# Attention and a routed feed-forward block on one core: a new order of score steps, first loads on GpSimd's queue, the guard as a bias column in one unit

## The chip, the core and the metric

The kernel runs on one core of a Trainium2 chip. A core has five engines with queues of their own: TensorE (PE, matmuls into PSUM), VectorE (DVE), ScalarE (ACT), GpSimd (POOL) and SyncE (SP), which here only issues DMAs. They meet at semaphores. A DMA is issued by SyncE or GpSimd and carried out by 16 DMA engines. The metric is the device time of one execution in microseconds (us).

## The reference

Four sequences of 1024 tokens, 256 channels. All inputs and the result are float32.

```python
qkv = x @ W_attn.T + b_attn                      # x: (4, 1024, 256)
q, k, v = split(qkv)                             # 16 heads of 16 channels
att = q @ k.T / sqrt(16) + rel_emb[bucket(distance)]
att = softmax(where(causal, att, -inf))
x = layernorm(x + (att @ v) @ W_proj.T + b_proj)
# then: gate scores pick one of 2 experts per token,
# relu(x @ w1[e] + b1[e]) @ w2[e] + b2[e], plus the term of the expert not picked (its input is zero)
# plus a shared expert; result = layernorm(x + sum)
```

The distance bias differs from a constant only where query and key are less than 256 apart, so it has to be added only in blocks near the diagonal.

## The kernel before

**Projection (project_in).** x comes in eight tiles of 512 tokens (two per sequence, t = 0 and 1). TensorE turns a tile (L644, from x_in), ScalarE and VectorE split it into a high and a low part (L491, L535), TensorE forms four blocks c of q and k from three products (L701) and then v (L663). ScalarE and VectorE split each q/k block into parts (L510, L581). SyncE stores the parts of a tile with four DMAs to qk_d in DRAM (store_tile, L412). GpSimd multiplies the high parts of q and k (selfs, L475), and one tile later TensorE sums squares and products into norms (L654, L656). parts has two buffers: before ScalarE writes a tile into one, the stores of the tile two earlier must have landed.

SyncE's queue is in order. For each tile n it issues the x load of tile n + 2 (L422, 512 KB), the four stores of tile n (2 MB together), and for tiles 1 to 4 two pieces of the skewed bias table bias_t (skew_bias, L406; 16 partitions, 256 rows of 1 KB each). After tiles 3 and 5 it loads the first two stacks (first_stack): a stack holds k in k_st and q in q_first or q_second for one unit of four heads, two sides of four DMAs (load_parts, L252 to L255), 32 or 16 partitions each, and two guard rows (load_guard, L272). first_stack first waits until all stores so far have landed.

**The guard.** From the norms and the largest bias the kernel derives a number that is subtracted from every score, so that no exponential overflows. VectorE writes it to neg_guard. In the first AP_UNITS units (2) of sequence 0 it goes into the exponential as a per-partition bias operand (L1061); in all others it lies in two extra rows of q, which are read from guard_d, and the exponential has no operand (L1059). guard_d is filled from guard_fill (L447, L449); for the first AP_UNITS units it holds zeros. The last tile's stores stand behind this fill and behind a branch that is decided on VectorE (ready.decided): an exact search for maxima, which is not taken with these inputs.

**Attention (attend).** 16 units: four sequences b by four groups g of four heads. A unit runs NSTEP = 9 steps, each with two pairs of heads. A step is one or two blocks (half of the queries, key block j, first query q, width w, column) that fill 512 columns for each head of the pair. For a pair, TensorE writes the scores to one of three PSUM slots (scores, L1151); if the step has a block near the diagonal, VectorE adds bias_t there, one instruction for each such block (L1117); ScalarE takes the exponential of 128 x 1024 values into probs; and TensorE multiplies by v and sums into o_ps (outputs, L1170). TensorE runs the scores two steps ahead. The steps' blocks are listed by hand in STEPS (L57 to L59). VectorE also copies each finished half of o_ps to o_sb (evacuate, L1078), at the places EVAC1 and EVAC0 (L902).

**Division and feed-forward.** The row sums are inverted (L1085), spread by DMA, and GpSimd multiplies y_t by them, one instruction per sequence (division.batch, L1230). That of the last sequence runs in the feed-forward stage, where ScalarE needs it for tile 6. There, TensorE forms the hidden layer (L2027) and the output (L2044), ScalarE and VectorE split the hidden layer (L1753, L1757, L1935: h_lo), VectorE computes the gate scores (L1784, an operation of x1 and gate_r, both in SBUF), GpSimd adds the residual's bias row (L1288) and scatters rows by indirect DMA (L1669).

## Time and profile before

| | us |
|---|---|
| median of 3 runs | 833.5 (833.4 to 835.99) |
| the profiled execution | 833.7 |
| its span, first to last instruction | 832.0 |
| PE busy | 777.1 (93%) |
| ACT busy | 542.7 (65%) |
| DVE busy | 514.6 (62%) |
| POOL busy | 243.5 (29%) |
| mean granted clock of TensorE | 0.976 of full speed |

Shares of the whole span mix three stages with different limits: the projection ends near 110 us, attention near 395, the rest is feed-forward. So the table only says where to look; which engine sets the pace is read stage by stage. A timeline row gives the start, the duration of a run of like instructions, the engine, the line of the kernel, what is written and read, the count, and in brackets the idle time before it with what ended that time.

### The profile page before, as it was taken

How to read it: one execution, taken by the hardware profiler on the slowest of the kernel's cores; microseconds unless marked ns; L12 is line 12 of the kernel's file. 1: busy time of each engine (PE TensorE's matmuls, PEld its weight loads, DVE VectorE, ACT ScalarE, POOL GpSimd, SP SyncE). 2: the span in 40 equal slices, each digit the busy share in tenths (PEclk: the TensorE clock that was granted, in tenths of full speed). 3: DMA queues.
4: the chain of work that ended last, by engine and by line, in shares of the span. 5: the costliest groups of instructions: out<-in, count | busy, mean ns of one | idle time of the engine just before them, and what ended most of it. 6: DMA issues, size and time to landing. Idle time of an engine off the chain costs nothing.

```text
span 832.0 us, 15414 instructions
## 1 busy us (share of the span) xinstructions
PE 777.1 (93%) x5761; PEld 556.8 (67%) x5761; DVE 514.6 (62%) x1120; ACT 542.7 (65%) x698; POOL 243.5 (29%) x199
## 2 busy tenths in 40 slices
PE   7994879999999999999979999999999999999993
PEld 6884633333334333343869988989899989999993
DVE  4662556666676666766886887886735445544453
ACT  5552659999999999999435556543444555555552
POOL 6221510000020021036154453443433232233332
PEclk9997979999999999999989999999999999999997
DMA  8899975577796699791582111201285334444300
GB/s 233 230 278 217 212 233 91 92 114 117 127 183 115 118 171 159 135 170 20 105 274 64 65 52 59 71 26 53 86 304 197 121 130 168 170 178 163 140 26 29
DMA packets 57878, 114.33 MB, mean 137 GB/s; under 512 B 7971, under 2 KB 35016, under 8 KB 55496
## 3 DMA queue, kind: packets, MB, share of 16 engines
...
## 4 chain that ended last, share of the span: by engine, by line
PE 74%; DVE 10%; ACT 7%; issue 4%; DMA 3%; POOL 1%; SPq 0%; POOLq 0%; DVEq 0%; ACTq 0%
PE slots L2027 19%; PE o_ps L1170 12%; PE slots L1151 11%; PE slots L2044 10%; PE o_ps L2044 10%; PE slots L701 4%; ACT probs L1059 4%; DVE slots L1117 3%; PE slots L1392 2%; ACT probs L1061 2%; DMA x_in<-L_attn_x 2%; PE o_ps L663 2%; DVE junk L1784 2%; PE slots L644 1%; DMA qk_d<-parts 1%
## 5 line engine op out<-in xcount | busy, mean ns | idle before, releaser
L1059 ACT ACTIVATE probs<-slots 128x1024 f32<-128x1024 f32 x252 | 237.6, 1037 | 5.6 <-DVE slots L1117 4.8
L1117 DVE TENSOR_TENSOR slots<-slots,bias_t 128x512 f32<-128x512 f32 (+1 forms) x288 | 160.3, 605 | 83.8 <-PE slots L1151 82.9
L1935 DVE TENSOR_TENSOR h_lo<-h_f,h_hi 128x512 fp32r<-128x512 f32 (+1 forms) x136 | 95.9, 706 | 106.5 <-PE o_ps L2044 62.4
L1170 PE MATMUL o_ps<-probs,v_st 128*32 128x512 f32 (+3 forms) x1664 | 154.6, 472 | 1.8 <-ACT probs L1059 0.4
L1753 ACT ACTIVATE h_f<-slots,b_cur 128x512 f32<-128x512 f32 (+1 forms) x72 | 47.9, 665 | 88.0 <-PE slots L2027 81.9
L1753 ACT ACTIVATE h_f<-slots,b_c 128x512 f32<-128x512 f32 x64 | 44.0, 687 | 73.6 <-PE slots L2027 65.4
L1757 ACT ACTIVATE h_hi<-h_f 128x512 fp32r<-128x512 f32 (+1 forms) x136 | 84.3, 620 | 4.3
L1151 PEld LDWEIGHTS slots<-q_first,k_st 50*128 50x128 f32 x416 | 34.7, 188 | 65.6 <-ACT probs L1059 43.5
L1151 PE MATMUL slots<-q_first,k_st 50*128 50x512 f32 (+3 forms) x416 | 69.0, 399 | 7.7 <-ACT probs L1059 2.7
L1151 PEld LDWEIGHTS slots<-q_second,k_st 50*128 50x128 f32 x416 | 34.0, 184 | 62.1 <-ACT probs L1059 44.4
L1170 PEld LDWEIGHTS o_ps<-probs,v_st 128*32 128x32 f32 x1664 | 39.9, 109 | 49.5 <-issue 30.2
L1151 PE MATMUL slots<-q_second,k_st 50*128 50x512 f32 (+3 forms) x416 | 67.7, 390 | 4.1 <-ACT probs L1059 2.6
L1708 POOL DMA_INDIRECT out<-o_out,id_i x32 | 35.7, 1116 | 103.3 <-DVE o_out L1899 96.0
L998 POOL COPY v_st<-v_all 128x512 f32<-128x512 f32 x16 | 9.8, 623 | 177.9 <-PE o_ps L1170 173.8
L1669 POOL DMA_INDIRECT base_d<-base,slot_i x32 | 40.9, 1279 | 48.1 <-DVE base L1877 40.4
L1669 POOL DMA_INDIRECT xs_d<-x,slot_i x32 | 34.3, 1073 | 62.5 <-DVE slot_i L1815 55.0
L2044 PE MATMUL slots<-shared_hi,h_hi 128*128 128x256 f32 x128 | 38.1, 298 | 6.4 <-DVE h_lo L1935 6.4
L2027 PE MATMUL slots<-x1t_lo,cur_hi 128*128 128x512 f32 (+1 forms) x144 | 43.3, 382 | 0.0
L2027 PE MATMUL slots<-x1t_hi,cur_lo 128*128 128x512 f32 (+1 forms) x144 | 43.3, 382 | 0.0
L2027 PE MATMUL slots<-x1t_hi,cur_hi 128*128 128x512 f32 (+1 forms) x144 | 43.2, 381 | 0.0
L2027 PE MATMUL slots<-x1t_hi,shared_hi 128*128 128x512 f32 x128 | 40.5, 398 | 1.2 <-ACT x1t_hi L1322 1.2
L2044 PE MATMUL slots<-experts_hi,h_hi 128*128 x144 | 41.2, 286 | 0.2
...
## 6 DMA issues: line engine op xcount, KB each, us to landing
...
```

What stands on the lines that cost most here:

```text
L701: ins = pe.matmul(slots[:, 1 + c // 2, c % 2], wq[w][:, kc, P * c:P * c + P], xt[a][:, t, kc, :], start=(i == 0 and kc == 0), stop=(i == 2 ...
L1059: nc.scalar.activation(dst, src, ACT.Exp).then_inc(exped, 1)
L1117: ins = dve.tensor_tensor(tile, tile, bias_t[:, h0:h0 + 2, first:first + w], ALU.add)
L1151: ins = pe.matmul(slots[:, k % SLOTS, h, col:col + w], k_st[at:at + KROWS, buf, pair, P * j:P * j + P], q_st[buf][at:at + KROWS, pair, q0: ...
L1170: ins = pe.matmul(o_ps[32 * j2:32 * j2 + 2 * D, half, q:q + w], v_st[:, g, j, j2, :], probs[:, (k + j2 // 2) % PBUFS, j2 % 2, col:col + w] ...
L1669: pool.indirect_dma_start(rows[:, :], bass.IndirectOffsetOnAxis(slot_i[:, t % 2, k:k + 1], 0), src[:, k, :], None).then_inc(done, 16)
L1708: pool.indirect_dma_start(out_rows[:, :], bass.IndirectOffsetOnAxis(id_i[:, j % 2, k:k + 1], 0), (o_out if j < EXP_TILES - 1 else y2)[:, k ...
L1753: nc.scalar.activation(h_f[:, q % 2, 0:w], l1_bank[q % 2][:, 0:w], ACT.Relu, bias=bias).then_inc(hf_ok, 1)
L1757: nc.scalar.activation(h_hi[:, n % 3, 0:w], h_f[:, q % 2, 0:w], ACT.Copy).then_inc(hh_ok, 1)
L1935: dve.tensor_tensor(h_lo[:, n % 3, 0:w], h_f[:, q % 2, 0:w], h_hi[:, n % 3, 0:w].bitcast(F32), ALU.subtract).then_inc(hl_ok, 1)
L2027: ins = pe.matmul(l1_bank[q % 2][:, 0:P * blocks(u)], w1_of(u, w)[:, kc, P * q:P * q + P], (xt_hi, xt_lo)[a][:, kc, 0:P * blocks(u)], star ...
L2044: ins = pe.matmul(acc_bank[k], (h_hi, h_lo)[a][:, n % 3, P * k:P * k + P], w2_chunk(u, w, q, e), start=(q == 0 and i == 0), stop=(q == HC ...
```

## The change

Five things are changed.

1. STEPS has a new order. Blocks of keys 1 and 2 of the second half are cut in 384 and 128 queries (LONG, SHORT), and no step holds two blocks near the diagonal any more. Nine steps stay nine. The place of EVAC0 moves one step ahead.
2. The bias pieces and the first two stacks are issued by GpSimd, between its products: four pieces after tiles 1 and 2, one side of a stack after tiles 3, 4, 5 and 6. They count on semaphores of their own (first_ld). SyncE's wait for the stores ahead of a stack goes; GpSimd waits for nothing new but pool_set, guard_out and dist_out.
3. AP_UNITS is 1: unit 1 has its guard in the extra rows.
4. Unit 1's guard rows are loaded by SyncE behind the fill of guard_d, after a wait for it (ready.guard_rows), in front of the last tile's stores.
5. The division of the last sequence is four instructions instead of one. Its reader waits for all four.

```diff
-STEPS = [[WHOLE[1][1]], [WHOLE[1][3]], [WHOLE[1][2]]] + [[x] for x in WHOLE[0]]
-STEPS += [[WIDE[0], NARROW[0]], [WIDE[1], NARROW[1]]]
-STEPS += [[MIDDLE[0], FAR_LEFT], [WHOLE[1][4]], [MIDDLE[1], FAR_RIGHT]]
+LONG, SHORT = ([(1, j, q, w, q) for j in (1, 2)] for q, w in ((0, TT - P), (TT - P, P)))
+STEPS = [[WHOLE[1][3]]] + [[x] for x in WHOLE[0]] + [[NARROW[0], LONG[0]], [MIDDLE[0], FAR_LEFT], [WIDE[0], SHORT[0]]]
+STEPS += [[WHOLE[1][4]], [MIDDLE[1], FAR_RIGHT], [WIDE[1], SHORT[1]], [NARROW[1], LONG[1]]]
...
-AP_UNITS = 2
+AP_UNITS = 1
...
-                    if 1 <= n <= P // SKEW // 2:
-                        skew_bias((2 * n - 2, 2 * n - 1))
-            def first_stack(g, b):
-
-                for t in range(TPB):
-                    sp.wait_ge(stored[t], 16 * NC * b)
...
-            body(0, False, True)
-            body(1, True, True)
-            first_stack(0, 2)
-            body(2, True, True)
-            first_stack(1, 3)
-            body(B - 1, True, False)
+            batches(sp, B - 1, body)
             sp.wait_ge(ready.fill, 2)
...
+            sp.wait_ge(ready.guard_rows, 32 * GUARD)
+            load_guard(sp, guard_d, 0, AP_UNITS, q_second, ready.guard_rows)
             sp.wait_ge(ready.decided, 1)
             store_tile(B - 1, TPB - 1)
 
         def gpsimd(pool):
+            def skew_bias(pieces):
+
+                pool.wait_ge(dist_out, 16)
+                for a in pieces:
+                    skew = bass.AP(bias_rows.tensor, P - SKEW * a, [[3 * P * H - 1, SKEW], [3 * P, H], [1, WIN]])
+                    pool.dma_start(bias_t[SKEW * a:SKEW * a + SKEW], skew).then_inc(bias_in, 16)
+
+            def first_stack(g, side):
+
+                q_st = (q_first, q_second)[g]
+                load_side(pool, *unit_rows(qk_d, 0, g), k_st[:, g], q_st, first_ld[g], side)
+                if side and g < AP_UNITS:
+                    load_guard(pool, guard_d, 0, g, q_st, first_ld[g])
+
+            def queue_loads(n):
+
+                if n in (1, 2):
+                    skew_bias(range(4 * n - 4, 4 * n))
+                if n == 3:
+                    pool.wait_ge(pool_set, 4)
+                    pool.wait_ge(guard_out, 16)
+                if 3 <= n < 7:
+                    first_stack((n - 3) // 2, (n - 3) % 2)
...
                         pool.tensor_tensor(selfs[:, c], parts[:, t, c, 0].bitcast(F32),
                                            parts[:, t, KC + c, 0].bitcast(F32), ALU.mult).then_inc(self_ok, 1)
+                    queue_loads(n)
...
-        EVAC1, EVAC0, INVERT = (1, 1), (NSTEP - 1, 1), (0, 1)
+        EVAC1, EVAC0, INVERT = (1, 1), (NSTEP - 2, 1), (0, 1)
...
-                    pe.wait_ge(st_ld[buf], 16 * ST_DMAS * (2 * b + g // 2 + 1))
+                    if first and g == AP_UNITS:
+                        pe.wait_ge(ready.guard_rows, 32 * GUARD + 32)
+                    if first and g < 2:
+                        pe.wait_ge(first_ld[buf], 16 * (ST_DMAS - GUARD * g))
+                    else:
+                        pe.wait_ge(st_ld[buf], 16 * ST_DMAS * (2 * b + g // 2))
...
-        y = y_t[:, :, bass.ds(b * T, T)]
-        pool.tensor_tensor(y, y, rs_row[:, :, :], ALU.mult).then_inc(step.y_norm, 1)
+        if b < B - 1:
+            y = y_t[:, :, bass.ds(b * T, T)]
+            pool.tensor_tensor(y, y, rs_row[:, :, :], ALU.mult).then_inc(step.y_norm, 1)
+            return
+        for t in range(TPB):
+            for kc in range(KC):
+                y = y_t[:, kc, bass.ds(b * T + TT * t, TT)]
+                ins = pool.tensor_tensor(y, y, rs_row[:, kc, TT * t:TT * t + TT], ALU.mult)
+                ins.then_inc(step.y_norm, 1)
```

Where the change moves instructions, their order was listed engine by engine. First SyncE's queue in the projection, from the stores of tile 3 on, before (qk_d<-parts are a tile's stores, bias_t<-bias_rows the bias pieces, the other qk_d rows a stack):

```order
L412 DMA qk_d<-parts 128x2x512 x4
L406 DMA bias_t<-bias_rows 16x16x256 x2
L252 DMA k_st<-qk_d 32x2x1024
L253 DMA k_st<-qk_d 16x2x1024
L254 DMA q_first<-qk_d 16x2x1024
L255 DMA q_first<-qk_d 32x2x1024
L252 DMA k_st<-qk_d 32x2x1024
L253 DMA k_st<-qk_d 16x2x1024
L254 DMA q_first<-qk_d 16x2x1024
L255 DMA q_first<-qk_d 32x2x1024
L272 DMA q_first<-guard_d 2x2x1024 x2
L422 DMA x_in<-L_attn_x 128x4x256
```

The same place of the changed kernel, from the stores of tile 3 to the end of the projection:

```order
L411 DMA qk_d<-parts 128x2x512 x4
L421 DMA x_in<-L_attn_x 128x4x256
L411 DMA qk_d<-parts 128x2x512 x4
L421 DMA x_in<-L_attn_x 128x4x256
L411 DMA qk_d<-parts 128x2x512 x8
L428 DMA guard_d<-guard_fill 128x96
L430 DMA guard_d<-guard_fill 128x3x128
L428 DMA guard_d<-guard_fill 128x96
L430 DMA guard_d<-guard_fill 128x3x128
L278 DMA q_second<-guard_d 2x2x1024 x2
L411 DMA qk_d<-parts 128x2x512 x4
```

Tile 6's x (the first L421) now follows tile 3's stores at once; only two small loads are new, in front of the last stores.

Second, GpSimd in the projection of the changed kernel, from its products of tiles 0 and 1 on (before, the products stood there alone):

```order
L482 TENSOR_TENSOR selfs<-parts 128x512 x4
L443 DMA bias_t<-bias_rows 16x16x256 x4
L482 TENSOR_TENSOR selfs<-parts 128x512 x2
L443 DMA bias_t<-bias_rows 16x16x256 x4
L482 TENSOR_TENSOR selfs<-parts 128x512 x2
L258 DMA k_st<-qk_d 32x2x1024
L259 DMA k_st<-qk_d 16x2x1024
L260 DMA q_first<-qk_d 16x2x1024
L261 DMA q_first<-qk_d 32x2x1024
L482 TENSOR_TENSOR selfs<-parts 128x512 x2
```

Between the two products of one tile and those of the next there are now four DMAs (six after tile 4).

Third, VectorE through one unit of attention before, from the copy of the unit before to the copy of its own first half and on to the next unit's:

```order
L1078 COPY o_sb<-o_ps 128x512
L1117 TENSOR_TENSOR slots<-slots,bias_t 128x2x256 x3
L1117 TENSOR_TENSOR slots<-slots,bias_t 128x2x128
L1117 TENSOR_TENSOR slots<-slots,bias_t 128x2x256
L1117 TENSOR_TENSOR slots<-slots,bias_t 128x2x128
L1117 TENSOR_TENSOR slots<-slots,bias_t 128x2x256
L1117 TENSOR_TENSOR slots<-slots,bias_t 128x2x128
L1117 TENSOR_TENSOR slots<-slots,bias_t 128x2x256
L1117 TENSOR_TENSOR slots<-slots,bias_t 128x2x128
L1117 TENSOR_TENSOR slots<-slots,bias_t 128x2x256 x6
L1078 COPY o_sb<-o_ps 128x512
L1117 TENSOR_TENSOR slots<-slots,bias_t 128x2x128 x2
```

The same engine and place of the changed kernel:

```order
L1086 COPY o_sb<-o_ps 128x512
L1125 TENSOR_TENSOR slots<-slots,bias_t 128x2x128 x2
L1125 TENSOR_TENSOR slots<-slots,bias_t 128x2x256 x10
L1086 COPY o_sb<-o_ps 128x512
L1125 TENSOR_TENSOR slots<-slots,bias_t 128x2x128 x4
L1125 TENSOR_TENSOR slots<-slots,bias_t 128x2x256 x2
```

There are 18 bias instructions in a unit as before, but now one for each of the 18 pairs; before, four pairs had two and four had none.

## Rows read from the trace of the kernel before

**Rows 1.** Windows: span, busy us (count) of PE, PEld, DVE, ACT, POOL; PEclk, DMA share, GB/s.

```profile
150.00:395.00 245.00, 236.82 (x2206) 94.72 (x2206) 162.80 (x284) 238.47 (x253) 39.67 (x24) 1.00 0.75 129
```

**Rows 2.** Waits of PE in 0 to 112 us: total, times, longest.

```profile
PE slots L644 <- DMA x_in<-L_attn_x: 15.4, 2, 10.6
```

**Rows 3.** Windows of 5 us in the projection.

```profile
55.00:60.00 5.00, 5.00 (x35) 4.46 (x33) 1.37 (x3) 3.97 (x6) 1.28 (x1) 1.00 1.09 360
...
70.00:75.00 5.00, 0.00 (x0) 0.00 (x0) 0.00 (x0) 0.00 (x0) 0.00 (x0) 0.74 1.05 138
```

**Rows 4.** Timeline of SyncE's queue (SPq).

```profile
52.47 1.03 SPq L406 DMA_DIRECT2D bias_t<-bias_rows  x2
60.34 0.32 SPq L252 DMA_DIRECT2D k_st<-qk_d  x1
```

**Rows 5.** The chain that ended last, 0 to 130 us: start, us, what.

```profile
37.50 0.87 PE slots L644 x8
38.38 2.81 PE o_ps L663 x24
...
64.62 13.45 DMA x_in<-L_attn_x
...
78.11 1.97 PE slots L644 x8
80.08 4.04 PE o_ps L663 x24
```

**Rows 6.** Timeline of GpSimd in the projection.

```profile
50.11 1.30 POOL L475 TENSOR_TENSOR selfs<-parts 128x512 bf16<-128x512 f32 x1 [1.90 <-ACT parts L510]
56.94 1.28 POOL L475 TENSOR_TENSOR selfs<-parts 128x512 bf16<-128x512 f32 x1 [5.53 <-ACT parts L510]
...
102.89 1.14 POOL L1276 DMA_DIRECT2D b_c<-L_ffn_sb  x1
```

**Rows 7.** Timeline of ScalarE at the start of attention.

```profile
111.31 1.11 ACT L1061 ACTIVATE probs<-slots,neg_guard 128x1024 f32<-128x1024 f32 x1 [2.56 <-PE slots L1151]
...
114.85 4.13 ACT L1061 ACTIVATE probs<-slots,neg_guard 128x1024 f32<-128x1024 f32 x4 [0.97 <-DVE slots L1117]
...
122.56 28.44 ACT L1061 ACTIVATE probs<-slots,neg_guard 128x1024 f32<-128x1024 f32 x28 [0.27 <-DVE slots L1117]
```

**Rows 8.** Timeline of one unit of attention, ScalarE, VectorE and TensorE.

```profile
174.05 3.95 ACT L1059 ACTIVATE probs<-slots 128x1024 f32<-128x1024 f32 x4 [0.18 <-DVE slots L1117]
...
177.10 3.39 DVE L1117 TENSOR_TENSOR slots<-slots,bias_t 128x512 f32<-128x512 f32 x6 [0.16 <-PE slots L1151]
...
178.17 13.07 ACT L1059 ACTIVATE probs<-slots 128x1024 f32<-128x1024 f32 x14 [0.17 <-DVE slots L1117]
178.55 0.50 PE L1151 MATMUL slots<-q_second,k_st 50*128 50x256 f32 x4
...
180.68 0.91 PE L1151 MATMUL slots<-q_second,k_st 50*128 50x512 f32 x4
...
181.22 1.30 DVE L1117 TENSOR_TENSOR slots<-slots,bias_t 128x512 f32<-128x512 f32 x2 [0.73 <-PE slots L1151]
...
184.47 0.91 PE L1151 MATMUL slots<-q_first,k_st 50*128 50x512 f32 x4
...
191.41 1.03 ACT L1059 ACTIVATE probs<-slots 128x1024 f32<-128x1024 f32 x1 [0.17 <-DVE slots L1117]
```

**Rows 9.** Timeline of the feed-forward stage, GpSimd, VectorE and TensorE.

```profile
421.02 4.67 POOL L1230 TENSOR_TENSOR y_t<-y_t,rs_row 128x2048 f32<-128x2048 f32 x1 [23.09 <-DMA rs_row<-rsum_d]
...
421.14 4.83 DVE L1784 CUSTOM_DVE_ANT_0 junk<-x,gate_r 128x256 f32<-128x256 f32 x1
...
426.01 2.44 DVE L1784 CUSTOM_DVE_ANT_0 junk<-x,gate_r 128x256 f32<-128x256 f32 x1
...
428.49 0.42 DVE L1784 CUSTOM_DVE_ANT_0 junk<-x,gate_r 128x256 f32<-128x256 f32 x1
...
430.05 0.58 PE L2044 MATMUL slots<-shared_hi,h_hi 128*128 128x256 f32 x1 [5.17 <-DVE h_lo L1935]
```

44 lines of the change are left out of this document (18 added, 26 removed).

## The prediction

> **What bounds the kernel now.** I read the windows by stage first, then the waits, then the chain. There are three stages: projection to about 110 us, attention to 395, feed-forward to 832. In attention ScalarE is busy 238.5 of 245 us, more than any engine [rows 1], so its exponentials set the pace there and every microsecond that they wait is lost. In the projection TensorE sets the pace, 10.0 us per tile, and waits long only once: 10.6 us, for an x tile [rows 2]. That is a matter of the DMA: it moves 360 GB/s while whole tiles are stored, but 138 GB/s, just as busy, while narrow loads are in its queue (the skewed bias with 16 partitions, the stacks with 16 or 32) [rows 3]. Feed-forward is TensorE's but for one place, where it waits 5.17 us for VectorE [rows 9].
>
> **Term 1, SyncE's queue in the projection.** SyncE has issued tile 3's stores and two bias pieces by 53.5, then stands until 60.3, until those stores have landed, because the first stack reads what was stored [rows 4]. It issues the ten DMAs of that stack, then tile 6's x at 64.6, which lands 13.45 us later, behind the stack [rows 5]. TensorE wanted it at 67.5 (78.11 - 10.6). Its clock then comes back late: 0.74 granted in the window inside the stall [rows 3], the turn takes 1.97 for 0.87 and the values 4.04 for 2.81 [rows 5]. The stall costs 10.6 + 1.1 + 1.2 = 12.9 us.
>
> After the change x of tile 6 can be issued at about 52.5, right behind tile 3's stores. But what GpSimd issues instead must still be moved. By shapes, a bias piece is 0.26 MB, one side of a stack 0.79 MB, a tile's stores and x together 2.6 MB. At the rates of [rows 3] that is 1.9, 5.7 and 7.3 us of DMA (5.8 for the stores, 1.5 for x). GpSimd issues four bias pieces (7.6 us of DMA) after tiles 1 and 2 each, and one side after each of tiles 3 to 6. With SyncE's 7.3 us this makes 13 to 15 us of work in every 10 us, so both queues stay backlogged from about 31.4 us on (tile 1's products end there, 20 us before tile 3's [rows 6]). If each gets half of the time, SyncE's work up to tile 6's x (stores of tiles 2 and 3, three x: 16.0 us, and some 1.5 left over) ends at 31.4 + 2 x 17.5 = 66.4, in time. Tile 7's x is 7.3 us of work later: 81.0, for 77.5. The stores of tiles 3 to 5 land up to 5 us after ScalarE wants to overwrite their buffer; TensorE needs those results only a step later, which covers most. So 3.5 us of the 12.9 stay, and the term is **-9.4**. Bounds: all 12.9 gone; or nothing, if GpSimd's work always goes first: eight pieces and three sides are 32.3 us, and 31.4 + 32.3 + 24.8 = 88.5 puts tile 7's x 11 us late, the stall of now.
>
> GpSimd's own time is hidden while four issues fit its pauses around the two products of a tile, 5.53 and 1.90 us [rows 6]. A DMA issued there took 1.14 us (1024 elements of 4 bytes; no row has one of these shapes): four are 4.6, the six with guard rows 6.8. With that cover gone, TensorE's norms wait for the products (rival C).
>
> **Term 2, start of attention.** VectorE is free for a bias only some 0.4 us before 114.85, after its branch. Now step 0 needs no bias: its two activations run from 111.31, and only the third waits for VectorE [rows 7]. Afterwards step 0 has a bias block too, so those two come behind 114.85: 2 x 1.11 = **+2.2**. Bounds: +1 (there are gaps behind the third that may absorb some) and +3.5 (TensorE idles longer and its clock rises later).
>
> **Term 3, the bias operand is gone in unit 1.** With it 28 activations took 28.44 us, (28.44 - 1.1)/27 = 1.012 us each [rows 7], so a unit of 18 takes 18.2 us. Unit 1 then runs as in term 4, 16.85: **-1.35**. Unit 0 stays at 18.2.
>
> **Term 4, the new order of steps, units 2 to 15.** A unit takes 17.36 us (174.05 to 191.41). Its last 14 activations follow each other at (13.07 - 1.03)/13 = 0.926 us, the first four at (3.95 - 1.03)/3 = 0.973, and two waits of 0.17 end on VectorE, each costing 1.03 + 0.17 - 0.926 = 0.27 [rows 8]. That is 0.14 + 0.54 lost; without them a unit takes 16.67. The cause is seen on VectorE: from 177.10 six instructions take 3.39 us, two of 0.65 and between them the two blocks of each pair of a double step, so 1.04 a pair [rows 8], more than ScalarE's 0.926. Afterwards every pair has one block, 0.65 at most. Against it: now all nine steps pass VectorE, where two did not. The ring of three slots bounds that: from one step's first scores (180.68) over bias, exponential, the next step's second pair and the sums to the first scores two steps on (184.47) is 3.79 us [rows 8], so nine such steps are 17.06. Three of the nine have the short 128-wide block, two of them behind the copies out of o_ps. I take the middle of 16.67 and 17.06, 16.85: 0.51 x 14 = **-7.1**. Bounds: 14 x 0.30 = 4.2 and 14 x 0.69 = 9.7. TensorE gets 8 more score matmuls and 8 more output matmuls a unit, of the same columns in all. A pair of four score matmuls occupies 0.50, a pair of two 0.45 [rows 8], so 2 steps x 2 pairs x 0.05 = 0.2 us a unit, hidden while ScalarE binds, 3.2 us in all if not.
>
> **Term 5, the last division in four.** GpSimd's division begins at 421.02; VectorE's gate operation, begun 0.12 later, takes 4.83 instead of 0.42, the next 2.44 beside GpSimd's residual [rows 9]. One operation slips in behind each GpSimd instruction. With four parts of about 1.2, one gate operation passes behind each, and only h_lo meets the residual: TensorE would get h_lo about 1 us earlier. Since that hangs on the phase, I take **-0.5**, bounds -1.5 and +1. The Trainium skill (SBUF — State Buffer, Who interferes with whom) says that when VectorE reads two SBUF inputs and GpSimd reads SBUF, the one that comes later "fully blocks" for the other's whole instruction. The row agrees for VectorE; if GpSimd too were held by each of four gate operations, the residual would end 1.7 us later, and this term would be +0.4.
>
> At nothing: unit 1's guard rows and tile 7's stores behind them. Their readers, the scores of unit 1 and the stacks of unit 2, come a unit later and more (over 16 us); what is queued behind SyncE's wait is only that.
>
> **Sum.** -9.4 + 2.2 - 1.35 - 7.1 - 0.5 = -16.2. The profiled execution took 833.7 (its span 832.0), the median of the runs is 833.5: **817.5**, a span of about 816.
>
> **Rivals.** *A, the DMA work binds, not its order.* The narrow loads are the same bytes; if theirs go first, term 1 is nil: 833.7 - 6.7 = 827. For it: 138 GB/s while they move, at a full DMA share. Against: half of the time is enough for SyncE. The Trainium skill (DMA: Bandwidth & Descriptors, Issuing engines are not separate DMA queues) says that DMAs issued by different engines end on the same 16 DMA engines and that issuing from several saves only the time to issue. By it, A and 827; the projection's trace has one queue and can't tell. *B, the loop over VectorE binds attention.* If a unit stays at 17.36, terms 3 and 4 shrink to -0.85: 825.1. For it: VectorE is now in every step. Against: the loop of 3.79. *A and B together:* 834.6, no change. *C, slower: GpSimd's issue time.* If such a DMA holds GpSimd for c us, a tile needs 4c + 2.6 us there, and TensorE's norms wait from c = 1.85 on. Six such tiles lose 6 x (4c - 7.4); from c = 2.65 the whole is slower than before by over 2.5 us, at c = 2.9 it is 843. The 1.14 speaks against it; the 256 runs of 1 KB in a bias piece are its case. *D, the change does more:* both bounds good, 810.
>
> **Chances.** Forecast 0.62 (its own range 811 to 823), A 0.16, B 0.11, A and B 0.04, C 0.05, D 0.02. The range, 810.5 to 827, takes in A and B. A measurement tells about 0.3%, 2.5 us, from no change. Faster by more: 0.91 (forecast, A, B, D); within it: 0.04; slower: 0.05.
>
> **What would show it.** Term 1: TensorE's wait for x_in is 3 us or less and SyncE no longer waits for stores; in A the wait stays near 10; in C TensorE's norms wait for selfs. Term 2: the first exponential starts with the first bias, near the end of the branch. Term 4: 16.7 to 17.1 us a unit, and ScalarE's waits on VectorE shorter. Term 5: gate operations of about 1.3 us beside each part. The forecast is wrong if two DMA queues side by side move less than one after the other, or if a unit takes over 17.1.

## The result

The changed kernel takes 828.36 us (median of 20 runs), the kernel before 834.19 us beside it (20 runs): 5.8 us less by the medians. The means, 830.2 and 834.1, are 3.9 us apart, and the ratio is theirs: 0.9953, interval [0.9934, 0.9972]. The forecast was 817.5, 16 us less, and the range ended at 827.0, so the time lies above it. The runs of the changed kernel fall into two groups: 16 between 826.7 and 831.8 us, 4 between 835.5 and 836.9. Its profiled execution, with a span of 834.1 us, is one of the second group, and part of what follows is why. One run of h4_both below took 1209.9 us at a mean granted clock of 0.557, where all others of this study have 0.97 to 0.98, and is left out.

Attention as a whole, in the view of windows, beside [rows 1]:

```profile
150.00:395.00 245.00, 239.97 (x2542) 107.22 (x2544) 161.85 (x283) 237.70 (x253) 38.70 (x23) 0.99 0.78 129
```

TensorE has gone from 236.8 to 240.0 us of 245, with 336 more matmuls; ScalarE's busy time is what it was.

**The projection**, beside [rows 2] to [rows 5]: TensorE's wait for x over the same 0 to 112 us (total, times, longest), its chain, and what GpSimd issued.

```profile
PE slots L652 <- DMA x_in<-L_attn_x: 13.0, 2, 8.1
```

```profile
41.70 23.18 DMA x_in<-L_attn_x
64.89 0.04 issue
64.94 1.97 PE slots L652 x8
66.91 4.17 PE o_ps L671 x24
```

```profile
30.57 2.54 POOL L443 DMA_DIRECT2D bias_t<-bias_rows  x4
...
40.59 2.25 POOL L443 DMA_DIRECT2D bias_t<-bias_rows  x4
...
50.60 0.56 POOL L258 DMA_DIRECT2D k_st<-qk_d  x1
```

The stall has only moved by one tile: x of tile 5, issued at 41.70, landed 23.18 us later, and TensorE waited 8.1 us for it instead of 10.6 for tile 6. The slow restart (1.97 and 4.17 us) is the one of [rows 5]. GpSimd took 0.6 us to issue a DMA, far from the 1.85 at which it would have mattered: rival C is out.

The x load was not alone in being late. ScalarE stood still longer than TensorE, for the stores of tile 2, before it could write tile 4's parts into the same buffer; the prediction had allowed up to 5 us for such waits, and for tiles 3 to 5 alone. SyncE's stores of tile 3 (SPq is SyncE's queue) stretched over it.

```profile
63.63 0.69 ACT L518 ACTIVATE parts<-slots,qk_bias 128x512 fp32r<-128x512 f32 x1 [13.69 <-DMA qk_d<-parts]
```

```profile
44.38 15.82 SPq L411 DMA_DIRECT2D qk_d<-parts  x4
```

How much of the 8.1 us would have gone with x alone in time, no run shows.

**Attention**, beside [rows 7] and [rows 8]: ScalarE's timeline from the start to the end, then VectorE's copy in it, and the chain just ahead of that copy.

```profile
111.73 6.14 ACT L1069 ACTIVATE probs<-slots,neg_guard 128x1024 f32<-128x1024 f32 x6 [5.98 <-DVE slots L1125]
119.17 2.12 ACT L1069 ACTIVATE probs<-slots,neg_guard 128x1024 f32<-128x1024 f32 x2 [1.31 <-DVE slots L1125]
122.19 2.12 ACT L1069 ACTIVATE probs<-slots,neg_guard 128x1024 f32<-128x1024 f32 x2 [0.90 <-DVE slots L1125]
125.30 8.14 ACT L1069 ACTIVATE probs<-slots,neg_guard 128x1024 f32<-128x1024 f32 x8 [1.00 <-DVE slots L1125]
133.29 134.55 ACT L1067 ACTIVATE probs<-slots 128x1024 f32<-128x1024 f32 x142
271.20 3.77 ACT L1067 ACTIVATE probs<-slots 128x1024 f32<-128x1024 f32 x4 [3.36 <-DVE slots L1125]
276.43 1.94 ACT L1067 ACTIVATE probs<-slots 128x1024 f32<-128x1024 f32 x2 [1.46 <-DVE slots L1125]
279.10 115.61 ACT L1067 ACTIVATE probs<-slots 128x1024 f32<-128x1024 f32 x122 [0.73 <-DVE slots L1125]
```

```profile
270.13 0.69 DVE L1086 COPY o_sb<-o_ps 128x512 f32<-128x512 f32 x1 [3.67 <-DMA sums<-o_sb]
```

```profile
257.76 12.25 DMA sums<-o_sb
```

142 activations in a row take 134.55 us: (134.55 - 1.03)/141 = 0.947 us each, 17.04 us a unit of 18. At 271.20 that row breaks. At the start of the third sequence VectorE's copy of half 0 stands 3.67 us for the DMA that takes the row sums out of the buffer it writes, and the biases behind it on VectorE stand too. Without the break the activation of 279.10 would have come at 133.29 + 148 x 0.947 = 273.4: 5.7 us are lost. The prediction did not have this wait at all. The change asks for this copy one step earlier (NSTEP - 2 for NSTEP - 1), in a unit that is shorter.

**Feed-forward**, beside [rows 9]: the division in four, VectorE's gate operations beside it, and TensorE's next work.

```profile
421.53 5.78 POOL L1249 TENSOR_TENSOR y_t<-y_t,rs_row 128x512 f32<-128x512 f32 x4 [22.55 <-DMA rs_row<-rsum_d]
```

```profile
421.82 1.52 DVE L1804 CUSTOM_DVE_ANT_0 junk<-x,gate_r 128x256 f32<-128x256 f32 x1
...
423.38 1.39 DVE L1804 CUSTOM_DVE_ANT_0 junk<-x,gate_r 128x256 f32<-128x256 f32 x1
```

```profile
430.40 0.58 PE L2064 MATMUL slots<-shared_hi,h_hi 128*128 128x256 f32 x1 [4.85 <-DVE h_lo L1955]
```

**Where the time of the profiled execution went.** Points in the two traces: the matmul that spreads the top norms (end of the projection's critical part), 105.28 before and 102.28 after; the first activation of unit 1, 132.69 (122.56 + 10 x 1.012) and 133.29; TensorE's first matmul behind attention, 395.10 and 395.77; the matmul above, 430.05 and 430.40; the end, 832.0 and 834.1.

| term | forecast | this profile | how |
|---|---|---|---|
| 1, projection | -9.4 | -3.0 | 102.28 - 105.28 |
| 2, start of attention | +2.2 | +3.6 | 31.01 - 27.41 from the top norms to unit 1 |
| 3, unit 1 without the operand | -1.35 | -1.2 | 17.04 for 18 x 1.012 |
| 4, the other 14 units | -7.1 | -4.5 | 14 x (17.04 - 17.36) |
| wait for the sums | none | +5.7 | above |
| 5, division | -0.5 | -0.3 | 34.63 - 34.95 from attention's end to h_lo |
| rest of feed-forward | 0 | +1.8 | 403.7 - 401.9 |

The sum is +2.1, the difference of the two spans. Whether the last row is the change's is open. In the profiles below the same stretch takes 401.6 to 402.4 us in the three with the old order of steps (e3, e4, h1), and 401.6 to 404.8 in those with the new one, three of which (f3, g1, g2) lie at 401.6 to 401.8. The first row varies too, from 101.1 to 104.6 us in seven profiles with these loads, so it is taken from several profiles below.

### The profile page after: what moved, and what is told of

Its sections match the earlier page's. It is cut to its first block, busy times and chain, and to the rows that moved or that the text cites. A ratio compares the mean times of both kernels' runs of the same rounds, so it can differ in the third digit from the quotient of the medians.

```text
span 834.1 us, 16183 instructions
## 1 busy us (share of the span) xinstructions
PE 783.3 (94%) x6145; PEld 571.4 (69%) x6145; DVE 516.6 (62%) x1120; ACT 540.0 (65%) x698; POOL 258.0 (31%) x228
## 4 chain that ended last, share of the span: by engine, by line
PE 78%; DVE 8%; DMA 5%; ACT 4%; issue 3%; POOL 1%; SPq 0%; POOLq 0%; DVEq 0%; ACTq 0%
PE slots L2047 19%; PE o_ps L1183 15%; PE slots L1164 13%; PE slots L2064 10%; PE o_ps L2064 10%; PE slots L709 4%; DMA x_in<-L_attn_x 3%; PE slots L1412 2%; ACT probs L1067 2%; PE o_ps L671 2%; DMA sums<-o_sb 1%; DVE junk L1804 1%; DVE slots L1125 1%; DVE h_lo L1955 1%; PE slots L652 1%
## 5 line engine op out<-in xcount | busy, mean ns | idle before, releaser
L1067 ACT ACTIVATE probs<-slots 128x1024 f32<-128x1024 f32 x270 | 254.3, 1032 | 7.2 <-DVE slots L1125 5.6
L1125 DVE TENSOR_TENSOR slots<-slots,bias_t 128x512 f32<-128x512 f32 (+1 forms) x288 | 163.5, 607 | 92.7 <-PE slots L1164 88.7
L1955 DVE TENSOR_TENSOR h_lo<-h_f,h_hi 128x512 fp32r<-128x512 f32 (+1 forms) x136 | 99.9, 737 | 106.3 <-PE o_ps L2064 56.5
L1183 PE MATMUL o_ps<-probs,v_st 128*32 128x384 f32 (+3 forms) x1920 | 158.1, 439 | 0.5 <-ACT probs L1067 0.3
L1164 PEld LDWEIGHTS slots<-q_first,k_st 50*128 50x128 f32 x480 | 39.1, 193 | 61.3 <-ACT probs L1067 37.3
L1183 PEld LDWEIGHTS o_ps<-probs,v_st 128*32 128x32 f32 x1920 | 47.2, 110 | 46.3 <-issue 29.1
L1164 PEld LDWEIGHTS slots<-q_second,k_st 50*128 50x128 f32 x480 | 37.8, 186 | 57.5 <-ACT probs L1067 44.5
L1164 PE MATMUL slots<-q_first,k_st 50*128 50x128 f32 (+3 forms) x480 | 71.2, 382 | 6.3 <-ACT probs L1069 3.2
L1164 PE MATMUL slots<-q_second,k_st 50*128 50x128 f32 (+3 forms) x480 | 69.2, 372 | 4.1 <-ACT probs L1067 2.7
L518 ACT ACTIVATE parts<-slots,qk_bias 128x512 fp32r<-128x512 f32 x32 | 21.9, 685 | 32.8 <-PE slots L709 18.7
```

Of the source, the lines that this page charges most:

```text
L1067: nc.scalar.activation(dst, src, ACT.Exp).then_inc(exped, 1)
L1125: ins = dve.tensor_tensor(tile, tile, bias_t[:, h0:h0 + 2, first:first + w], ALU.add)
L1164: ins = pe.matmul(slots[:, k % SLOTS, h, col:col + w], k_st[at:at + KROWS, buf, pair, P * j:P * j + P], q_st[buf][at:at + KROWS, pair, q0: ...
L1183: ins = pe.matmul(o_ps[32 * j2:32 * j2 + 2 * D, half, q:q + w], v_st[:, g, j, j2, :], probs[:, (k + j2 // 2) % PBUFS, j2 % 2, col:col + w] ...
L1955: dve.tensor_tensor(h_lo[:, n % 3, 0:w], h_f[:, q % 2, 0:w], h_hi[:, n % 3, 0:w].bitcast(F32), ALU.subtract).then_inc(hl_ok, 1)
```

## The experiments

**Parts of the change by themselves.** Four kernels: the order of steps, everything but the early copy, the loads, the division.

e1_steps, the kernel before with

```
+LONG, SHORT = ([(1, j, q, w, q) for j in (1, 2)] for q, w in ((0, TT - P), (TT - P, P)))
+STEPS = [[WHOLE[1][3]]] + [[x] for x in WHOLE[0]] + [[NARROW[0], LONG[0]], [MIDDLE[0], FAR_LEFT], [WIDE[0], SHORT[0]]]
+STEPS += [[WHOLE[1][4]], [MIDDLE[1], FAR_RIGHT], [WIDE[1], SHORT[1]], [NARROW[1], LONG[1]]]
-        EVAC1, EVAC0, INVERT = (1, 1), (NSTEP - 1, 1), (0, 1)
+        EVAC1, EVAC0, INVERT = (1, 1), (NSTEP - 2, 1), (0, 1)
```

> The kernel before with the new order of steps alone (and the copy of half 0 one step earlier, as the change has it). Theory 1, TensorE is the new bound: a unit of attention takes 17.05 us as in the changed kernel (17.36 before), TensorE being busy over 99% of it, because two steps of a unit now have four score matmuls a pair for two. 14 x 0.31 = -4.3 us, the start of attention +3.6, so about -0.7 us, or up to +7 where the copy of half 0 at the start of the third sequence waits for the sums' DMA. Theory 2, the forecast's: 16.85 us a unit and +2.2 at the start, -4.9 us in all. The end of the projection (first matmul that spreads the top norms, 105.28 us before) stays where it was in both.

Measured: 832.32 us (828.9 to 836.5), ratio 0.9968 [0.9946, 0.9991], 1.6 us below the kernel before (833.89). ScalarE's row in its profile:

```profile
150.93 117.63 ACT L1059 ACTIVATE probs<-slots 128x1024 f32<-128x1024 f32 x124
270.51 3.77 ACT L1059 ACTIVATE probs<-slots 128x1024 f32<-128x1024 f32 x4 [1.95 <-DVE slots L1117]
...
278.60 115.58 ACT L1059 ACTIVATE probs<-slots 128x1024 f32<-128x1024 f32 x122 [0.92 <-DVE slots L1117]
```

The unit is (117.63 - 1.03)/123 x 18 = 17.06 us, the number of theory 1 (what binds it is tried below), and the break stands at the same place (the copy waits 2.26 us for the sums), without any of the moved loads: 278.60 is 4.4 us later than the unbroken row would have it. From the top norms (103.36) to unit 1 (120.69 + 12 x 1.014 = 132.86) it is 29.5 us for 27.4: here the start costs 2.1. So the new order with its early copy makes both the gain of term 4 and the new wait.

e2_evac_last, the changed kernel with

```
-        EVAC1, EVAC0, INVERT = (1, 1), (NSTEP - 2, 1), (0, 1)
+        EVAC1, EVAC0, INVERT = (1, 1), (NSTEP - 1, 1), (0, 1)
```

> The changed kernel with the copy of half 0 out of o_ps back behind the last step (NSTEP - 1 for NSTEP - 2). Theory 1: in the profiled execution of the changed kernel that copy stood 3.67 us for the DMA of the sums at the start of the third sequence, with the slow restart behind it some 7 us in all, and this is what parts its runs into some near 828 and some near 836. A step later the copy asks 1.9 us later, so the wait shrinks to under 2 us or is gone: the runs lie together, highest under 832, the median near 827.5. Theory 2, the runs above 835 have another cause (a whole execution that is slower): they appear here too, about one in four. Theory 3, the earlier copy was needed: TensorE waits for o_ps at each unit's start, 0.3 us x 15, and the median rises by 4 us or more.

Measured: 827.21 us, six runs between 826.4 and 829.6, ratio 0.9918 [0.9897, 0.9938]. In its profile the copy waits 0.26 us for the sums and the row of activations never breaks:

```profile
133.82 255.65 ACT L1067 ACTIVATE probs<-slots 128x1024 f32<-128x1024 f32 x270
```

All 15 units at (255.65 - 1.03)/269 x 18 = 17.04 us. TensorE did not need the earlier copy (theory 3 is out).

e3_loads, the changed kernel with the steps, the copy and the division of before (so the loads, AP_UNITS = 1 and the guard rows are what remains of the change):

> The kernel before with only the loads moved: bias pieces and first stacks on GpSimd's queue, one unit with the bias as an operand, the guard rows of unit 1 fetched by SyncE; steps, copies and division as before. Theory 1, the DMA engines' work binds the projection, as their share of 1.0 from 35 to 95 us says: the wait for x_in only moves from tile 6 to tile 5 and is 8 us long, the top norms are spread at 102.3 (105.3 before), -3.0 us, and with unit 1 at 17.36 for 18.2, -0.9, the time is 3.9 us below the kernel before. Theory 2, the forecast's: the wait for x_in is 3 us or less and the time 10 us below.

Measured: 831.49 us, ratio 0.9965 [0.995, 0.998], 2.4 us below the kernel before. Top norms at 102.36 us, TensorE's waits for x some 8 us. Theory 1 in kind; it gives less than the 3.9, since the projection gains less than the 3.0 us of one pair of profiles (table below).

e4_division, the kernel before with

```
+        if b < B - 1:
...
+        for t in range(TPB):
+            for kc in range(KC):
+                y = y_t[:, kc, bass.ds(b * T + TT * t, TT)]
+                ins = pool.tensor_tensor(y, y, rs_row[:, kc, TT * t:TT * t + TT], ALU.mult)
```

> The kernel before with only the last division split in four. Forecast: VectorE's gate operations take 1.2 to 1.5 us each for one of 4.83, TensorE gets h_lo 0.3 to 0.5 us earlier counted from the end of attention (34.88 us before), and the time is 0.3 us below the kernel before, within what the runs can tell. Rival, both engines are held by each other in turn: the residual ends 1.7 us later and TensorE gets h_lo 0.4 us later.

Measured: 834.28 us, ratio 1.0001 [0.9987, 1.0015]: nothing that a time can show. The rows say more. From attention's first following matmul to the h_lo matmul it is 34.95, 34.94 and 34.94 us in three of the four profiles with one division, and 34.61 to 34.64 in ten with four: -0.3. In this kernel's own profile it was 31.55, in e2's and g2's 32.5 and 36.1, where the gate operations fell otherwise on GpSimd's instructions; as the prediction said, that hangs on the phase. GpSimd's four parts took 5.78 us in the changed kernel, its one division 4.67 [rows 9]. Not all of these 1.1 us need be a hold by VectorE: single GpSimd instructions of 128 x 512 took 1.28 us (L1746) and 1.29 (L482), four of them some 5.1, so some 0.7 is left for it.

**Term 4: what binds a unit at 17.04.** TensorE is busy 16.9 of every 17.0 us in the changed kernel (16.45 before), so it looks like the bound. The prediction had offered another: the ring of three slots through VectorE, 17.06. Two kernels with work left out tell them apart; both stand on e2_evac_last.

f1_narrow_bias:

```
                                 for col, w, first in near(STEPS[s]):
+                                    w = min(w, P)
                                     tile = slots[:, k % SLOTS, :, col:col + w]
```

> The changed kernel with the copy of half 0 behind the last step, and VectorE adding the bias to the first 128 columns alone of each block (the rest of the bias is left out). An activation now follows the other every 0.947 us, a unit takes 17.04. Theory 1, TensorE binds a unit (busy 16.9 of every 17.0 us in the changed kernel, 16.45 before): the same 17.04 us, the time within 1 us of the kernel with the whole bias (827.2 median). Theory 2, the ring of three slots through VectorE binds it, as the upper bound of term 4 (17.06) has it: VectorE's instructions go from 0.65 to 0.43 us, the loop of 3.79 us over two steps has two of them and shrinks by 0.4, and a unit falls to ScalarE's own 16.67: 15 x 0.37 = 5.5 us less.

f2_less_sums:

```
-                pieces = PIECES[s]
+                pieces = [x for x in PIECES[s] if not (x[0] == 1 and x[1] in (1, 2) and x[3] == P)]
```

> The changed kernel with the copy of half 0 behind the last step, and the output matmuls of the two short blocks (128 columns, left of the diagonal) left out: 2 x 4 of 128 columns a unit, some 2 x 0.25 us of TensorE's 16.96. Theory 1, TensorE binds: a unit falls from 17.04 towards ScalarE's own 16.67 (18 x 0.926), 16.6 to 16.75, so 15 x 0.35 = 5 us less and VectorE and ScalarE see no new waits. Theory 2, the ring through VectorE binds: those sums stand in the ring for 0.25 us in two of nine steps only, a unit falls by 0.1 to 0.3.

Measured: ScalarE's row of f1, then of f2.

```profile
130.09 132.70 ACT L1067 ACTIVATE probs<-slots 128x1024 f32<-128x1024 f32 x144
265.00 116.08 ACT L1067 ACTIVATE probs<-slots 128x1024 f32<-128x1024 f32 x126 [2.22 <-DVE slots L1126]
```

```profile
130.95 253.72 ACT L1067 ACTIVATE probs<-slots 128x1024 f32<-128x1024 f32 x270
```

With VectorE's instructions at 0.43 us for 0.65 a unit takes (132.70 - 1.03)/143 x 18 = 16.57 us; with less work for TensorE alone 16.91. Theory 2 both times: VectorE's part of the ring binds. The single activations of e2_evac_last between 151 and 190 us agree: one begins 0.90 to 0.92 us after the other, but four times a unit, about once in two steps, it is 1.03 to 1.11, and each of these begins 0.03 us behind VectorE's instruction. So the ring binds, though VectorE is busy only two thirds of the time, and TensorE's 99% is no evidence, as the windows from 151 to 253 us of e2_evac_last and of f1_narrow_bias show (in the order of [rows 1]):

```profile
151.00:253.00 102.00, 101.45 (x1084) 45.43 (x1080) 69.15 (x122) 101.43 (x109) 8.23 (x7) 1.00 0.81 132
```

```profile
151.00:253.00 102.00, 101.73 (x1106) 46.96 (x1104) 52.71 (x124) 102.00 (x112) 8.22 (x7) 1.00 0.85 133
```

TensorE did 2% more matmuls in the same 102 us when VectorE got shorter. So 99.5% busy was not the most that it could do; that the difference is waiting which the record counts as work is the likely reading. The units of f1 are so short that the copy waits 2.83 us for the sums even behind the last step, the break at 265.00. Times of the two: 823.8 and 826.0 us (two runs each).

g3_sums_between changes TensorE's own place in that ring (it stands on g1_second_behind, below):

```
-                    for pair in range(PAIRS):
-                        ahead(b, i + 2, pair, before, after)
-                    outputs(b, i, before)
+                    ahead(b, i + 2, 0, before, after)
+                    outputs(b, i, before)
+                    ahead(b, i + 2, 1, before, after)
```

> As g1_second_behind, with TensorE's order in a step changed: scores of the first pair, output matmuls, scores of the second pair (for both scores, then outputs). Theory 1, the ring of three slots binds a unit (17.04 us; with narrower bias additions it took 16.57): the scores of the first pair of the next step no longer stand behind the outputs, but those of the second pair do; if that shortens the loop, a unit takes 16.6 to 16.8, 15 x 0.35 = 5 us less. Theory 2, it lengthens the loop for the second pair by the outputs' 1.0 us: 17.5 and more a unit, 7 us and more slower.

Measured: 832.54 us against 819.44 for g1_second_behind. A unit takes 17.86 us (from one row to the next):

```profile
128.30 17.05 ACT L1071 ACTIVATE probs<-slots 128x1024 f32<-128x1024 f32 x18 [0.81 <-DVE slots L1129]
146.16 17.05 ACT L1071 ACTIVATE probs<-slots 128x1024 f32<-128x1024 f32 x18 [0.81 <-DVE slots L1129]
```

The number is theory 2's (17.5 and more), the mechanism is not. Within a unit the pace has not changed: (17.05 - 1.03)/17 = 0.942 us an activation for 0.947. Nearly all of the loss is the one wait of 0.81 us between units, 15 x 0.81 = 12 of the 13.1 us. There TensorE's first output matmuls of a unit stand for VectorE's copy out of o_ps, and now the second pair's scores stand behind them:

```profile
144.10 1.07 PE L1187 MATMUL o_ps<-probs,v_st 128*32 128x512 f32 x8 [1.02 <-DVE o_sb L1090]
```

In all TensorE stands 15 times for that copy, 15.4 us; in g1_second_behind it does so nowhere. So g3 prices a wait at the edge of a unit, and says nothing on what binds inside one.

**Term 1: the order of the queues or the DMA's work.** All of these have the copy behind the last step; only GpSimd's list of loads differs, or where the second stack is issued.

f4_pieces_spread:

```
-                if n in (1, 2):
-                    skew_bias(range(4 * n - 4, 4 * n))
+                if 1 <= n <= 4:
+                    skew_bias((2 * n - 2, 2 * n - 1))
```

> The changed kernel with the copy of half 0 behind the last step, and the eight bias pieces issued two after each of tiles 1 to 4 instead of four after tiles 1 and 2; stacks as in the change. Theory 1, the DMA work binds: the same bytes, so the stall for x_in only moves to a later tile; top norms spread at 102 to 105 us, time within 1 us of the kernel that differs in the copy alone (827.2). Theory 2, the burst of four narrow pieces ahead of x of tile 5 causes the stall: it vanishes, top norms at 96 to 98 us, time 5 us less.

f3_second_stack_late, beside the lines of f4:

```
-                if 3 <= n < 7:
-                    first_stack((n - 3) // 2, (n - 3) % 2)
+                if n in (5, 6):
+                    first_stack(0, n - 5)
+                if n == TILES - 1:
+                    first_stack(1, 0)
+                    first_stack(1, 1)
```

> The changed kernel with the copy of half 0 behind the last step; bias pieces two after each of tiles 1 to 4, the first stack after tiles 5 and 6, and the whole second stack (1.5 MB in 8 DMAs) only after tile 7. Theory 1, the work of the DMA engines binds the projection: 1.5 MB, 8 to 11 us of DMA at the rates 360 and 138 GB/s, go out of it, so the waits for x_in fall from 8 to under 3 us and the top norms are spread at 98 to 99 us (102.3, 104.6 and 102.4 in three profiles with the changed loads), 4 to 5 us less in all. Theory 2, the order of the queues matters, not the work: as the kernel that spreads the pieces alone.

Measured: f4 827.67 us, no different from e2_evac_last (827.21); its stall is one tile later again, 5.54 us before 72.59, and the top norms come at 100.66, between what the two theories said. f3 822.65 us, no wait for x at all, top norms at 92.46, 10 us earlier. That is more than theory 1 said (98 to 99), and f3 also has the first stack two tiles later than the change. But the first exponential came at 106.17, 13.7 us behind the top norms instead of 9.4. VectorE stood in its branch; the chain and the timeline of f3:

```profile
98.33 7.13 issue
```

```profile
105.65 1.36 DVE L1128 TENSOR_TENSOR slots<-slots,bias_t 128x256 f32<-128x256 f32 x3 [6.59 <-issue]
```

g1_second_behind, beside f3:

```
-                if n == TILES - 1:
-                    first_stack(1, 0)
-                    first_stack(1, 1)
             sp.wait_ge(ready.decided, 1)
+            for t in range(TPB):
+                sp.wait_ge(stored[t], 16 * NC)
+            for side in range(2):
+                load_side(sp, *unit_rows(qk_d, 0, 1), k_st[:, 1], q_second, first_ld[1], side)
             store_tile(B - 1, TPB - 1)
```

> As f3_second_stack_late, but the second stack is issued by SyncE behind the branch (after its wait for the decision) instead of by GpSimd after tile 7. In f3 the top norms were spread at 92.5 us with no wait for x_in at all, but VectorE then stood 7.13 us in its branch, where it stands 2.9 us in the other kernels, and the first exponential came 13.7 us behind the top norms instead of 9.4. Theory 1, the code of the branch is fetched through the DMA engines behind the 1.5 MB of the second stack: with the stack behind the branch VectorE stands 2.9 us again, first exponential at 102, time 4 us below f3's 822.65. Theory 2, the longer stand has another cause: it stays near 7 us and the time is f3's. Against both: the stack must land before unit 1's first scores, some 15 us later; if it takes longer, TensorE waits there by up to 5 us.

Measured: 819.44 us (816.3 to 822.6), ratio 0.9829 [0.9797, 0.9862]. VectorE's stand is 2.22 us again:

```profile
101.19 1.36 DVE L1129 TENSOR_TENSOR slots<-slots,bias_t 128x256 f32<-128x256 f32 x3 [2.22 <-issue]
```

and the second stack lands in time, with no wait of TensorE at unit 1. The view of the DMA queues between 97 and 106 us shows what stood in the way: first f3, then g1. One packet of instructions is fetched there in either, and takes 2.5% of 16 engines' 9 us, 3.6 us, for 0.9%, 1.3 us.

```profile
q8 instruction: 1, 0.02, 2.5%
```

```profile
q8 instruction: 1, 0.02, 0.9%
```

The same view of narrower windows has the packet whole at 100.9 to 104.6 us in f3 and at 97.7 to 99.2 in g1:

```profile
q8 instruction: 1, 0.02, 6.1%
```

```profile
q8 instruction: 1, 0.02, 5.6%
```

VectorE goes on 0.9 us behind it in f3 (105.46) and 1.8 in g1 (101.00). That it is this packet for which VectorE stood is the reading that fits both; the trace has no row that ties the two.

h2_burst_late, g1_second_behind with the change's own burst (`if n in (1, 2): skew_bias(range(4 * n - 4, 4 * n))`, first stack at `n in (3, 4)`), and h1_before_late, the kernel before with the second stack behind the branch:

```
             body(2, True, True)
-            first_stack(1, 3)
             body(B - 1, True, False)
...
             sp.wait_ge(ready.decided, 1)
+            first_stack(1, 3)
             store_tile(B - 1, TPB - 1)
```

> g1_second_behind with the change's own order of the other loads: four bias pieces after tiles 1 and 2 each, the first stack after tiles 3 and 4; only the second stack behind the branch. Theory 1, the stall for x of tile 5 comes from what has been queued by 50 us (eight pieces and one side of the first stack, 2.9 MB), which is the same here as in the changed kernel: a wait of 7 to 8 us at 57 to 65 us stays, top norms at 99 to 101 us, the time 7 us above g1's 819.4. Theory 2, the 1.5 MB of the second stack alone decide: no wait, top norms at 92.4, the time of g1.

> The kernel before with the second stack issued by SyncE behind the branch instead of before tile 7's wait (94.0 us in its trace); one queue, all else as before. The stall for x of tile 6 (10.6 us, at 67 to 78) comes before the second stack is issued, so it stays, and the projection gains nothing before 94: top norms at 103.5 to 105.5 us (105.3, 103.4, 104.0 in three profiles of that projection), the time within 1.5 us of the kernel before. Rival, DMA work of any place counts: 5 us and more below it.

Measured: h2 829.96 us, ratio 0.9955 [0.9927, 0.9984]; h1 832.15 us, 0.9975 [0.9956, 0.9994] (before: 833.71). TensorE's rows behind the stall, of h2 and of h1:

```profile
65.36 1.97 PE L656 MATMUL slots<-ident,x_in 128*128 128x128 f32 x8 [8.11 <-DMA x_in<-L_attn_x]
```

```profile
77.90 1.97 PE L644 MATMUL slots<-ident,x_in 128*128 128x128 f32 x8 [10.50 <-DMA x_in<-L_attn_x]
```

Both as theory 1 had them as to the stall; the top norms of h2 came at 104.61, later than its 99 to 101, so taking the second stack away after the stall gave nothing that this profile shows. Put together, top norms by profile:

| loads of bias and first stack | second stack before tile 7's end | behind it |
|---|---|---|
| one queue (before) | 105.3, 103.4, 104.0 | 105.0 (h1) |
| GpSimd's, in a burst (the change) | 102.3, 104.6, 102.4, 101.1, 101.5, 104.2, 103.7 | 104.6 (h2) |
| GpSimd's, pieces spread | 100.7 (f4, first stack after tiles 3 and 4) | 92.5, 92.4, 93.6, 92.7 (first stack after tiles 5 and 6) |

Term 1 of the change is the second row's mean less the first's: 102.8 - 104.2 = -1.4 us. The last cell differs from f4 by the stacks alone, the second out of the way and the first two tiles later. It differs from h2 by the spreading and by the later first stack, and from h1 by the second queue and by the later first stack. So what is shown is that the stacks' places matter. The later first stack stands in every difference and was never tried by itself, nor was one queue with it: whether the second queue or the spreading is needed at all stays open.

g2_warm, g1_second_behind with ten matmuls of 512 columns into o_ps in TensorE's idle time between projection and first exponential, `warm(3)` ahead of the second scores and `warm(7)` ahead of the fourth:

> As g1_second_behind, with ten more matmuls of 512 columns into o_ps (a bank that the first sums overwrite) in TensorE's idle time between the projection and the first exponential. Theory 1, part of the cost at the start of attention is TensorE's clock: granted 0.50 there, an output step takes 1.86 us instead of 1.00 and up to three of them do (after's profile), so with the clock at 1.0 some 2 to 3 us go. Theory 2, the extra matmuls do not raise the clock or are in the way: no change or up to 2 us slower.

Measured: 818.71 us, ratio 0.9809 [0.9778, 0.984], not to be told from g1. The windows of g2 from 95 us on:

```profile
95.00:100.00 5.00, 2.61 (x13) 1.54 (x12) 4.42 (x15) 1.69 (x3) 1.74 (x3) 0.90 0.05 5
100.00:105.00 5.00, 4.71 (x13) 3.07 (x13) 1.57 (x4) 1.98 (x2) 0.11 (x1) 0.50 0.36 107
105.00:110.00 5.00, 4.71 (x24) 2.13 (x24) 1.84 (x4) 4.15 (x5) 0.00 (x0) 0.50 1.01 156
110.00:115.00 5.00, 4.83 (x38) 1.88 (x36) 2.81 (x5) 3.65 (x4) 0.00 (x0) 0.73 1.04 153
```

TensorE was busy 4.7 of 5 us and the granted clock stayed at 0.50 (1.2 GHz) all the same: it had fallen before, between 95 and 100, where TensorE was busy 2.6 of 5 us. Theory 1 falls; the clock comes back no earlier than in g1. In windows of 1 us it is first 1.00 at 110 to 111 in g1, and at 113 to 114 in g2, whose top norms come 1.2 us later.

**The two groups of runs.** g4_sums_gpsimd is the changed kernel with `move_sums(b - 1, ...)` taken from SyncE's list and its four DMAs issued by GpSimd behind `load_v(b, UNITS - 1)`. h3_shared_late is the changed kernel with

```
                 if before:
                     fetch_sums(sp, b - 1)
+                if not after:
+                    load_shared(0)
+                    load_shared(1)
...
-                if 1 <= b <= 2:
-                    load_shared(b - 1)
```

and h4_both is g1_second_behind with the same.

> The changed kernel, copy of half 0 at NSTEP - 2 as the change has it, with the row sums (16 KB, four DMAs) of each sequence moved by GpSimd's queue instead of SyncE's. Theory 1, the copy's wait of 3.67 us is the sums standing behind a unit's stack and 1 MB of shared weights in SyncE's queue (12.25 us from the last issue to the landing, under 8 us at the other two sequences): on a queue of their own they land within 5 us, VectorE never waits for them, the runs lie together near 828 with none above 832. Theory 2, they wait for the DMA engines' work whatever the queue: the wait and the runs above 835 stay.

> The changed kernel (copy of half 0 at NSTEP - 2) with the two 1 MB loads of the shared weights, issued by SyncE in the second and third sequence ahead of the unit's stack, both moved to the last sequence. Theory 1, the sums of the third sequence land late (12.25 us) because the 1 MB (18.8 us from issue to landing in the changed kernel's profile, 12.2 before) has pushed the whole queue back: they land within 8.5 us at every sequence, VectorE never waits for them, and all runs lie below 832. Theory 2, the upper group has another cause: one run in four above 835.

> g1_second_behind with both 1 MB loads of the shared weights in the last sequence. In g1 the copy of half 0 did not wait for the sums in its profile, its runs are 816.3 to 822.6. Theory 1, the loads matter only by the copy's wait: same median as g1 (819.4) within 1 us, spread under 4 us. Theory 2, the 2 MB now meet the fetch of the x rows and the last sums and delay the first matmuls of the feed-forward part: 2 us slower.

Measured: g4 830.54 us, 12 runs between 827.1 and 839.7, three of them above 835; h3 828.88 us, six runs between 827.8 and 830.0, ratio 0.993 [0.9903, 0.9957]; h4 817.7 us, five runs between 816.5 and 819.5, ratio 0.9797 [0.9767, 0.9828]. In the profiles of g4 and h3 the copy never waits for the sums. h3 comes out as theory 1 has it, but by few runs: were one run in five still slow, six would show none with a chance of 0.26. h4's median lies 1.7 us below g1's 819.4, more than the 1 us of its theory 1, and its runs within g1's. g4 does not come out so: on a queue of their own the sums landed in time in its profiled execution, yet three of its twelve runs are still some 8 us slower. In h2, whose copy stands behind the last step, the copy still waited 1.42 us and one run of ten took 837. So the wait for the sums is shown as the cause in the profiled execution (5.7 of its 7.5 us above the median), and e2, f4 and h3 have 18 runs, none above 830.0 (0.8 to the 18th is 0.02). That it is the cause of every slow run is not shown, and the kernel before has single runs at 836 to 840 as well.

## Why the prediction was wrong, point by point

**Term 1, -9.4 forecast, -1.4 measured: the largest miss (8 us), rival A's.** The step that failed is the sum behind "if each gets half of the time": that half of the time lets SyncE's queue through its work in twice the time that it takes alone. By the prediction's own prices SyncE had 10.3 us of work up to tile 5's x at 31.4 us (1.5 left over, the x of tile 4, tile 2's stores, 1.5 for x of tile 5), 3.7 MB at 360 GB/s. Twice that makes 52.0, in time for 56.8. If GpSimd's eight pieces (15.2) and the first side of a stack (5.7) all go first, it is 31.4 + 31.2 = 62.6. It landed at 64.9. The view of the DMA queues shows packets, MB and share of time of GpSimd's queue (q0) and SyncE's (q1), first for 31.4 to 52.0, then for 31.4 to 64.9 us:

```profile
q0 software_dynamic: 507, 1.69, 52.7%
q1 hardware_dynamic: 1529, 2.47, 50.7%
```

```profile
q1 hardware_dynamic: 2992, 4.79, 53.3%
q0 software_dynamic: 896, 2.88, 50.1%
```

So SyncE did have half of the time. But up to 52.0 it moved 2.47 MB in it, 237 GB/s of its own time for 360, and x of tile 5 had not come. By 64.9 all of GpSimd's 2.88 MB (eight pieces and one side) had been moved, and 1.1 MB more of SyncE's than the work up to that x. At the prediction's prices these bytes are 20.9 and 13.3 us, together 34.2 for the 33.5 that passed: the prices hold for the sum of the queues, not for one of them beside the other. Even the first side of the stack, issued at 50.6, 9 us behind that x, landed 8.6 to 10.5 us later, ahead of it. The prediction also began its sums at tile 6; tile 5, the first x behind the burst, was not looked at. Its allowance of 5 us for stores that hold up ScalarE was short as well: that wait was 13.69 us. The rule that stood beside rival A, of the Trainium skill (DMA: Bandwidth & Descriptors, Issuing engines are not separate DMA queues), that several issuers end on the same 16 engines, agrees with the window of the stall, in which the engines were busy throughout:

```profile
57.00:65.00 8.00, 0.07 (x1) 0.07 (x2) 0.65 (x1) 1.28 (x3) 0.00 (x0) 0.66 1.05 309
```

Taken alone it does not say when a load lands: f3 and g1, with the same two queues, have no stall.

**Term 2, +2.2 forecast: right.** From the top norms to unit 1 the kernels with the new order take 29.5 (e1), 29.3 (e2), 29.1 (g1) and 29.1 to 29.2 us (f4, g4, h3), those with the old one 27.4, 27.2, 26.9 and 27.2: +2.0. In the profiled execution of the changed kernel it was 31.0, just beyond the upper bound of +3.5 that the prediction gave for a clock that rises later. Its chain has three output steps of 1.86 us there, where they take 1.00 at full clock; that these are the difference was not tried.

**Term 3, -1.35 forecast, -1.2 measured: right,** short of it by what unit 1 shares of term 4's miss.

**Term 4, -7.1 forecast, -4.5 measured: mechanism right, size at the pessimistic end.** Both bounds were named, 16.67 and 17.06; the middle was taken, and the unit is 17.04. The lower one was ScalarE's own pace, the upper the ring, nine times the loop of 3.79 us over 2. The step that was mis-sized is the middle: there was no reason for it, since a loop of 3.79 us is longer than two of ScalarE's steps, and all nine steps pass through it. The argument for less, shorter VectorE instructions in three of nine steps, did not show in the sum; why was not tried. f1 shows that the ring is through VectorE. The prediction also counted 8 more output matmuls a unit where there are 16 (1376 before and 1592 after between 150 and 380 us, 13.2 units), with the 8 more of the scores. They are nearly hidden: without a quarter us of output matmuls in two steps (f2) a unit is 0.13 shorter.

**Term 5, -0.5 forecast, -0.3 in the rows: right in size,** and invisible in the time. The rule of the Trainium skill that stood there (SBUF — State Buffer, Who interferes with whom) would have GpSimd held too. The prediction worked that out as 1.7 us, which would have turned the sign. The four parts took 1.1 us more than the one division, of which some 0.7 can be a hold: less than by that rule.

**What was priced at nothing and was not.** The copy one step earlier. The prediction said of the copies only that they keep a place behind their sums; it did not ask what else the copy waits for. Its line has two waits on DMAs (y_out and sum_in), and at the third sequence the sums had 10.5 us from the first one's issue to the copy (255.93 to 266.46, where it was due) for 13.0 before (258.46 to 271.42), behind a stack and 1 MB of shared weights in SyncE's queue. In the profiled execution that cost 5.7 us, more than all of term 4 gave.

**The sum.** -1.4 + 2.0 - 1.2 - 4.5 - 0.3 = -5.4 without the wait for the sums; 834.2 - 5.4 = 828.8 for the measured median of 828.4. The agreement proves little of the single terms: the feed-forward row of the table is left out, and no profile was taken of a run in the lower group. The sign was right, as forecast with a chance of 0.91. The range missed by 1.4 us because its upper end took in A or B, each alone, but not A nearly whole with a third of B (2.7 of its 7.6 us), which is what happened.
